# A four-layer kernel: stacked single-pass scores in the second attention, and a written order for the norms behind the experts

## The reference, cut to what matters

```python
xn = _ln(x, g1, b1)
q = _lin(xn, Wq, bq).reshape(b, n, H, HD) / np.sqrt(HD)
k = _lin(xn, Wk, bk).reshape(b, n, H, HD)
score = jax.nn.softmax(jnp.einsum('bihd,bjhd->bhij', q, k), axis=-1)
v = _lin(xn, Wv, bv).reshape(b, n, R, HD)
out = jnp.einsum('bhij,bjrd->bihrd', score, v)
...
comp = jax.nn.softmax(comp, axis=3)
out = (comp * out).sum(axis=3).reshape(b, n, DIM)
```

## Time and profile before

| | us |
|---|---|
| median of three runs (1006.62, 1006.65, 1010.5) | 1006.65 |
| the profiled execution | 1010.96 |
| its span | 1009.2 |
| TensorE busy in the span | 747.9 |
| VectorE busy | 578.9 |
| ScalarE busy | 455.0 |
| GpSimd busy | 84.6 |
| mean granted TensorE clock (1 is 2.4 GHz) | 0.814 |

### The profile page before, as it was taken

The page is one execution under the profiler, slowest core; times in us unless marked ns, Lnnn a source line. Parts: engine busy times, 40 slices in busy tenths (PEclk is TensorE's granted clock), DMA queues, the critical chain, the costliest instruction groups (busy, mean ns, idle before and its releaser), DMA issues. The chain is left out here.

```text
span 1009.2 us, 15707 instructions
## 1 busy us (share of the span) xinstructions
PE 747.9 (74%) x5853; PEld 613.7 (61%) x5853; DVE 578.9 (57%) x1314; ACT 455.0 (45%) x936; POOL 84.6 (8%) x96
## 2 busy tenths in 40 slices
PE   3993869898942786536960379999999993748996
PEld 2443769896432466526860246888888983537875
DVE  4119999993475165323326644577777738465474
ACT  2332635452433545202534523555555541457584
POOL 0002203100000101051430010000000000100000
PEclk9996757796875688556995558999999996868998
DMA  5200170004101000012010030000000000000000
GB/s 165 34 0 1 23 123 2 1 3 169 77 1 64 1 1 1 1 37 71 30 53 16 1 117 1 2 2 1 0 0 1 2 1 1 0 1 1 1 22 21
DMA packets 27457, 26.43 MB, mean 26 GB/s; under 512 B 17424, under 2 KB 25488, under 8 KB 26624
## 3 DMA queue, kind: packets, MB, share of 16 engines
q1 hardware_dynamic: 26144, 22.99, 7.9%
q0 software_dynamic: 1248, 2.57, 0.8%
HBM read 20.32 MB, written 5.23 MB: 25 GB/s over the span
## 5 line engine op out<-in xcount | busy, mean ns | idle before, releaser
L2201 PE MATMUL PS<-VXT,PT 128*128 128x73 f32 (+1 forms) x1024 | 126.6, 277 | 4.8 <-ACT PT L2225 4.8
L2201 PEld LDWEIGHTS PS<-VXT,PT 128*128 128x128 f32 x1024 | 119.7, 192 | 17.0 <-issue 12.3
L2312 DVE TENSOR_REDUCE MX<-PS 128x2 f32<-128x512 f32 x128 | 81.8, 685 | 49.2 <-PE PS L2164 48.4
L2225 ACT ACTIVATE PT<-PS 128x512 f32<-128x512 f32 x128 | 68.6, 597 | 47.4 <-PE PS L2169 47.4
L2161 PE MATMUL PS<-Q,KZ 32*128 32x256 f32 x512 | 76.8, 397 | 0.0
L2164 PE MATMUL PS<-KZ,Q 32*128 32x256 f32 x512 | 74.2, 420 | 1.6 <-DVE MX L2312 1.5
L2169 PE MATMUL PS<-MR,SEL 32*128 32x256 f32 x256 | 58.8, 462 | 0.0
L2238 ACT ACTIVATE UB<-PS 128x292 f32<-128x292 f32 x64 | 26.6, 415 | 52.8 <-PE PS L2201 52.8
L2164 PEld LDWEIGHTS PS<-KZ,Q 32*128 32x128 f32 x512 | 46.3, 196 | 5.9 <-DVE MX L2312 3.8
L404 PE MATMUL PS<-XT,WT 128*128 x96 | 44.1, 616 | 1.0 <-ACT XT L290 1.0
L2161 PEld LDWEIGHTS PS<-Q,KZ 32*128 32x128 f32 x512 | 38.8, 184 | 5.7 <-issue 0.8
(11 more groups left out here) (465 smaller groups left out, 1782.4 us busy)
## 6 DMA issues: line engine op xcount, KB each, us to landing
PB<-in_pb SPq DMA_DIRECT2D x1, 5016.0 KB, 17.9
PB<-in_pd SPq DMA_DIRECT2D x1, 2888.0 KB, 9.9
X<-in_x SPq DMA_DIRECT2D x2, 1024.0 KB, 4.8
X<-fir_rows SPq DMA_DIRECT2D x2, 1024.0 KB, 6.6
TR<-fir_rows SPq DMA_DIRECT2D x2, 1024.0 KB, 8.7
PA<-in_pa SPq DMA_DIRECT2D x1, 1731.0 KB, 8.5
PC<-in_pc SPq DMA_DIRECT2D x1, 1560.0 KB, 6.5
by_expert<-ZERO_ SPq DMA_DIRECT2D x1, 1483.5 KB, 15.1
```

The costliest lines, as they stand in the source:

```text
L2201: last = nc.tensor.matmul(PS[:, UM.bank(n), col:col + VX], PT[:, k % 4, c, f * P:(f + 1) * P], v, start=(c == 0), stop=(c == 1))
L2225: nc.scalar.activation(PT[:, k % 4, :, :], PS[:, UM.bank(n), :].rearrange("p (c q) -> p c q", c=2), ACT.Exp).then_inc(c_act, 1)
L2312: nc.vector.tensor_reduce(MX[:, :, k], PS[:, UP_.bank(n), :].rearrange("p (f q) -> p f q", f=2), AX.X, ALU.max, negate=True).then_inc(p_dv ...
```

## The change

1. **Scores.** A float32 number is written as the sum of two float32r numbers, a high and a low part. ScalarE makes the high parts of q and k (`high_parts`), VectorE the low parts (`low_parts`); both stand in `HALVES`. Eight transfers a batch (`spread`, from SP) write them to `Q4` and `K4`, three buffers each: row 4d + c of a head's 32 rows is feature d, high or low by c, q and k in different order. One product over 32 rows then sums all four combinations of parts. `Q`, `KZ` and `take_projections` go; the weights' columns, their bias and the factor for q are rearranged to fit (`PERM`, `BC`, `BQK2`, `BS`).
2. **Order in a batch.** The projection for the batch after the next stands in step 0, the low parts in step 1; the projection's bank is the ring's third. Step 2's second max score goes to that bank and waits for both parts. The loop is gone: all batches are written out.
3. **Weighted product.** It multiplies 128 columns of `VXF`, which is `VXT` with a pad behind it; ScalarE copies 73 of each 128.
4. **Norms.** `WAVES` is replaced by an order written out by hand. For k = 2 ScalarE makes only `NRM`; the sixteen applies to `XL` stand behind the high parts of batch 1, in the attention's first round.
5. **Folding.** GpSimd makes `PERM` first; VectorE makes `BC` from the biases behind `SEL`; TensorE multiplies them ahead of the products with `BD`.

```diff
-        Q = [sbuf(s4, f"Q{n}", [P, L]) for n in range(2)]
-        KZ = [sbuf(s4, f"KZ{n}", [P, 4, L]) for n in range(2)]
+        arrived = lambda eng, b: eng.wait_ge(split_in[b % 4], 16 * COPIES * (b // 4 + 1))
...
+        def high_parts(act, bank, b):
+            act.wait_ge(split_full, b + 1)
+            if b:
+                arrived(act, b - 1)
+            for s_ in range(2):
+                nc.scalar.activation(HALVES[:, 2 * s_, :], bank[:, s_ * L:(s_ + 1) * L], ACT.Identity,
+                                     bias=BS[:, s_:s_ + 1]).then_inc(split_high, 1)
+
+        def low_parts(dve, bank, b):
+            dve.wait_ge(split_high, 2 * b + 2)
+            for s_ in range(2):
+                nc.vector.scalar_tensor_tensor(out=HALVES[:, 2 * s_ + 1, :], in0=bank[:, s_ * L:(s_ + 1) * L],
+                                               scalar=BS[:, s_:s_ + 1], in1=HALVES[:, 2 * s_, :], op0=ALU.add,
+                                               op1=ALU.subtract).then_inc(split_low, 1)
+
+        def spread(sp, b):
+            sp.wait_ge(split_high, 2 * b + 2)
+            sp.wait_ge(split_low, 2 * b + 2)
+            for to, plane_of in ((Q4, lambda c: c // 2), (K4, lambda c: 2 + c % 2)):
+                for c in range(4):
+                    sp.dma_start(to[b % 3][c:P:4, :, :].bitcast(F32),
+                                 HALVES[:, plane_of(c), :].bitcast(F32)).then_inc(split_in[b % 4], 16)
...
+                    nc.gpsimd.tensor_copy(PERM[:, :].rearrange("p (j d s) -> p j s d", j=4, s=4),
+                                          ident.rearrange("p (j s d) -> p j s d", j=4, s=4)).then_inc(c_perm, 1)
                     nc.gpsimd.memset(BD[:, :, :], 0.0).then_inc(c_zero, 1)
...
+                    pe.wait_ge(c_bias, 1)
+                    pe.wait_ge(c_perm, 1)
+                    nc.tensor.matmul(PS[:, 3, 8:10], PERM[:, :], BC[:, :],
+                                     start=True, stop=True)
                     pe.wait_ge(c_bd, 1)
...
                     V.link(nc.vector.tensor_copy(SEL[:, :], CRW[:, :]))
+                    nc.vector.tensor_tensor(BT[:, 0, :], pc("bq"), QT[:, :], ALU.mult)
+                    V.link(nc.vector.tensor_tensor(BT[:, 1, :], pc("bk"), QT[:, :], ALU.mult))
+                    nc.vector.tensor_reduce(BC[:, :], BT[:, :, :], AX.X, ALU.add).then_inc(c_bias, 1)
...
+                    root(0, 0)
+                    root(0, 1)
+                    apply(0, 0)
+                    root(0, 2)
+                    apply(0, 1)
+                    root(0, 3)
+                    apply(0, 2)
+                    root(1, 0)
...
+                    turned(1)
+                    high_parts(act, PS[:, 0, :], 0)
+                    apply(2, 2)
+                    turned(2)
+                    apply(2, 3)
+                    turned(3)
...
+                    begin(0, 0)
+                    begin(0, 1)
+                    middle(0, 0)
+                    begin(0, 2)
+                    middle(0, 1)
+                    begin(0, 3)
+                    end(0, 0)
+                    middle(0, 2)
+                    end(0, 1)
+                    middle(1, 0)
+                    end(0, 2)
+                    middle(0, 3)
+                    end(1, 0)
+                    middle(1, 1)
+                    end(0, 3)
+                    middle(2, 0)
+                    middle(1, 2)
+                    end(1, 1)
+                    middle(1, 3)
+                    end(1, 2)
+                    middle(2, 1)
+                    end(1, 3)
+                    middle(2, 2)
+                    values(0)
+                    middle(2, 3)
+                    low_parts(dve, PS[:, 0, :], 0)
+                    values(1)
+                    values(2)
+                    values(3)
...
-            prep = ROUND + [("qk", 0), ("turn", 0)]
+            prep = ROUND[0:2] + [("qk", 0)] + ROUND[2:] + [("turn", 0)]
...
+                for b in [None] + list(range(B)):
+                    after = 0 if b is None else b + 1
+                    last = after == B
                     for i in range(H2 // 2):
+                        scores(i, b, None if last else after)
+                        if i == 0 and after + 1 < B:
+                            project_next(after + 1)
+                        if i == 1 and after + 1 < B:
+                            split_next(after + 1)
...
+                                if n == at_p[("qk", 0)] + 4 and a + 1 < B:
+                                    pe.wait_ge(split_high, 2 * a + 4)
+                                    pe.wait_ge(split_low, 2 * a + 4)
...
-                                nc.tensor.matmul(PS[:, UM.bank(at_m[("exp", k)]), os], KZ[odd][rows_of(k), k // 4, cs],
-                                                 Q[odd][rows_of(k), :], start=True, stop=False)
+                                nc.tensor.matmul(PS[:, UM.bank(at_m[("exp", k)]), os], K4[b % 3][rows_of(k), k // 4, cs],
+                                                 Q4[b % 3][rows_of(k), k // 4, :], start=True, stop=False)
...
-                                col = ((k % 2) * 2 + f) * VX
+                                col = ((k % 2) * 2 + f) * P
...
-                                    v = VXT[:, bass.ds(b * 2 + c, 1), :].rearrange("p t c -> p (t c)")
+                                    v = VXF[:, (b * 2 + c) * VX:(b * 2 + c) * VX + P]
...
+                    def project_next(b):
+                        high_parts(act, PS[:, SPLIT_BANK, :], b)
+                        if b == 1:
+                            for t in range(NT):
+                                nc.scalar.activation(XL[:, t, :], X[:, t, :], ACT.Identity, bias=NMG[:, 0, t:t + 1],
+                                                     scale=R2S[:, 0, t:t + 1])
```

267 lines of the change are left out of this document (122 added, 145 removed).

## The result

The changed kernel took 978.45 us (median of four runs: 977.78, 978.19, 978.71, 984.77), the one before beside it 1008.58; the ratio is 0.971, with an interval of 0.9656 to 0.9764. On a second chip, in more runs, it was 983.25 against 1006.71, ratio 0.9767 (0.9725 to 0.9808). The forecast said 984.5, with 973 to 999 around it.

A forecast was written before the change was run, and what follows sets the result against it. TensorE was taken to bound the attention's batches, a VectorE-ScalarE chain the norms. Terms +2.2 - 15.9 - 1.5 - 10.2 = -25.4 us, with two dips -22, take the median from 1006.65 to 984.5 us; range 973 to 999.

The forecast's parts named there:

- Folding, +2.2: Ahead of the experts: TensorE's first product with BD waits behind the PERM product for the folded bias, costing 2.2 us.
- Norms, -15.9: Norms behind the experts: the new order and moving 16 applies to XL into the attention save 15.9 us.
- First scores, -1.5: Between the norms' warming products and the attention's first batch: the 25.6 us stretch gets 1.5 us shorter.
- Scores 0.7, weighted 2.0 a step: TensorE in each attention step: scores fall from 1.30 to 0.7 us, the weighted product goes from 1.94 to 2.0.
- The chain through VectorE: Attention batches: VectorE's path becomes the bound, 26.6 us a batch against 26.8, TensorE idling 1.8 and 1.9 us.
- Attention, -10.2 without dips: All attention batches: 182.7 us from first to last for 188.8, last batch 32.5 for 36.6; 10.2 us saved.
- ScalarE's table load, 1.3: Attention: 1.3 us added to the batch periods in the 182.7 us from the first to the last batch.
- The last batch, 32.5: End of the attention: without reductions it takes 8 x 2.7 + 10.9 for its finish, 32.5 us against 36.6.
- Two dips at 1.7: Inside the batches: TensorE's clock dips twice at 1.7 us each, taking the sum from -25.4 to -22 us.
- dips in most batches: Rival, attention: eight to twelve clock dips give back 14 to 20 us, total 995 to 1001; chance 0.20.
- the clock falls and stays: Rival, attention: clock stays at 1.2 GHz, such a batch costs 16 us more, four give 1046; chance 0.05.
- Transfers, 0: Attention: each batch's eight transfers from SP are hidden, cost 0; rival of late transfers, 1006 us, chance 0.03.

The follow-up runs named there:

- fold_behind: Changed kernel with the folded-bias product moved behind TensorE's products with BD, and the copy to PERM behind GpSimd's clear of BD; 981.43 us, executed once.
- scores_float32: Changed kernel with the same stacked score operands multiplied as float32, two instructions where the change has one; 1010.33 us, ratio 1.0007 to the kernel before.
- low_parts_thrice: Changed kernel with each low-part operation of batches 1 to 7 done three times on VectorE; 1009.58 us, ratio 1.0008 to the kernel before.
- low_step0: Changed kernel with VectorE's low parts in step 0, ahead of the finish's start, instead of step 1 behind it; 980.26 us, executed once.
- end_step1: Changed kernel with the finish's end, weigh and sum each one step earlier behind its start; 970.42 us, ratio 0.9625 to the kernel before.
- weighted_73: Changed kernel with the weighted product back at 73 columns and one dense copy by ScalarE; 1080.77 us, ratio 1.0677 to the kernel before.
- xl_in_norms: Changed kernel, written norm order kept, with ScalarE's sixteen applies to XL back inside the norms, in front of those to NRM; 996.19 us, executed once.

## Why the prediction was right

- **Folding, +2.2.** From the SEL copy to the first norm +2.0, to the experts' first product +1.9, and the reason was the one given: the wait for the folded bias, 2.09 us. fold_behind took 1.6 of it out. The terms as given, 462.7 + 0.4 - 460.74 - 0.3, make 2.1 and not 2.2.
- **Norms, -15.9.** -16.8; VectorE's waits at the end for TensorE's products are there (2.73 and 2.06). Where the last 0.9 comes from wasn't tested; a part of TensorE's products at the high clock (the window's mean is 0.54, the walk took 0.5) would do it. The split, 11.5 for the order and 5.3 for the applies, is shown from both sides.
- **First scores, -1.5.** -1.4 from the last value to the first batch, which is where the forecast cut it (22.17 + 4.22 before, 20.01 + 4.95 after). The table cuts at the first copy of `MR`, where it is -2.2; the warming products behind it lay 1.5 us longer at half the clock than before.
- **Scores 0.7, weighted 2.0 a step.** 0.67 and 1.98. The single pass behaves like the product with SEL, as taken; scores_float32 gives its worth, 24.1 us in all.
- **The chain through VectorE.** Gaps of 1.8 and 1.9 us were named, 1.73 and 2.00 came; the batch was forecast at 26.6 and takes 26.26, the first 23.8 and 23.45, the one before the last 24.6 and 24.24. low_parts_thrice, low_step0 and end_step1 show that it is this chain and not VectorE's work that sets the period.
- **Attention, -10.2 without dips.** From the first batch's start to the last one's it was 182.7 forecast and 182.76 measured, but the measured figure holds 3.8 us of dips, so that the two agree is chance. Two terms were wrong: each period was 0.35 too long (7 x 0.35 = 2.4), and ScalarE's table load, 1.3, was added on top of the first batch's 23.8, which took 23.45 with it. The load isn't free: most of what TensorE stands in that batch is the wait for the exponential behind it. The last batch, 32.5, took 32.6 (775.84 to 808.43).

```profile
593.89 1.28 ACT L2291 ACT_TABLE_LOAD   x1 [11.02 <-PE PS L2238]
...
596.42 2.02 PE L2269 MATMUL PS<-VXF,PT 128*128 128x128 f32 x16 [0.87 <-ACT PT L2291]
```

- **Clock.** Two dips at 1.7 were in the sum (3.4); three at 1.15 to 1.40 came (3.8). The Trainium skill (TensorE: Matmul & The Clock Gate, A second HAM failure mode: psum-queue depth-cycling) tells of a clock that swings between its levels as TensorE stands shortly between groups of products, which the prediction read as dips in most batches. The trace agrees that the short waits bring them, as they vanish once the gaps are filled, and only in part with that extent: of the five batches that have both gaps three had a dip. Two slips stand in the working: eight to twelve dips at 1.7 to 2 us are 14 to 24 and not 14 to 20, and the kernel before did have a gap longer than some tenths, the 1.73 us in its first batch.
- **The rival that should have weighed more.** Against "the clock falls and stays" the prediction argued that at the low clock TensorE has no gaps left, and so would get the clock back. weighted_73 refutes that argument: it has no gaps and stays at 0.50. What kept the changed kernel from it was the width of the weighted product, which the prediction priced at 0 to 0.1 us a step and mentioned only as making the batch denser. That the forecast held here, with 0.05 for this case, was luck: its reason was wrong.
- **Transfers, 0.** Shown, with about 12.5 us to spare.

The terms sum to -25.4, with dips -22; the stages gave -26.4 with dips, 3.3 of the difference in the attention. The early part, which no term speaks of, moved the profiled execution by another -7.3, and the medians differ by 23.5 to 30.1 us, by chip: how near the whole time came to 984.5 (978.45, and 983.25 on the second chip) is in part luck.

## What to carry to other kernels

When an engine's instructions are made cheaper, walk one period through all engines with rows of the trace and look at where the written order makes one engine stand for another: here 3.9 us a batch of TensorE's time were freed and 0.5 kept, until one line of the finish's schedule gave back two more. A cheaper instruction stream can also cost TensorE its clock, so columns that carry nothing can pay for themselves many times over (here about 100 us for 0.04 us a step), and an unused product in a gap a little (2.6 us); look at the granted clock in each stretch before such padding is taken out as waste. And compare stages cut at the same instructions, not whole times, where the code in front varies by more than the effect of one part, and look at the clock's stretches before a difference of 1 or 2 us is read from a stage.

## What the runs showed that was not expected

- In the profiled execution the single pass at 73 columns is granted 0.50 for 270 us on end while TensorE is busy over 99% of the time; at 128 columns, otherwise alike, 1.00 but for the dips.
- A wait that grows from 1.73 to 3.8 us on VectorE's account costs 4.28 us a period for 2.07 of work: the rest is clock.
- The stretches at half the clock inside batches are mostly of 3.4 us after gaps of 1.7 to 2, but 6.8 and 10.2 us came too, in low_step0 and xl_in_norms after gaps no longer than 2.1; 3.4 us of it cost 1.15 to 1.40 in the changed kernel, 0.8 to 1.6 elsewhere.
- Nearly the same code ahead of the change ended between 454.4 and 468.0 us from execution to execution.
